# Cross-attention on one core: mask counts of blocks 4 to 7 in the values' bank, the projection directly behind the scores in odd steps

## The reference

```
q = heads(x @ W_Q.T); k = heads(ctx @ W_K.T); v = heads(ctx @ W_V.T)
scores = q @ k.T / 4;  scores = where(mask == 1, -1e9, scores)
p = softmax(scores);  out = concat_heads(p @ v) @ W_O.T + x
result = (out - mean(out)) * rsqrt(var(out) + 1e-5) * gamma + beta
```

## Time and profile before

| | us |
|---|---|
| three runs | 182.85, 186.15, 188.56 (median 186.15) |
| the profiled execution | 182.77 |
| its span, first to last instruction | 181.0 |
| PE busy | 159.6 (88%) |
| DVE busy | 136.9 (76%) |
| ACT busy | 103.2 (57%) |
| POOL busy | 102.5 (57%) |
| mean granted clock of PE | 0.976 |

### The profile page before, as it was taken

How to read it: one execution, slowest core, us unless ns; L and a number is a source line. 1 busy time by engine, 2 the same in 40 slices (tenths; PEclk the granted TensorE clock), 3 DMA queues, 4 the chain that set the end, 5 groups by cost and what they waited for, 6 DMA issues and landing times.

```text
span 181.0 us, 3572 instructions
## 1 busy us (share of the span) xinstructions
PE 159.6 (88%) x1224; PEld 87.9 (49%) x1224; DVE 136.9 (76%) x305; ACT 103.2 (57%) x188; POOL 102.5 (57%) x125
## 2 busy tenths in 40 slices
PE   7698877889579999999999999999999897999830
PEld 7455534444244565456545654565366462264520
DVE  0779755885958579788978897889989966748990
ACT  3224154673366565658765876587777659586400
POOL 7000761242835451448597959754954787865692
PEclk9999999999999999999999999999999999699995
DMA  4949947779867987973686665647551033020205
GB/s 158 384 120 184 257 86 224 182 167 230 188 170 217 281 237 216 253 201 85 196 274 181 193 198 145 187 164 205 141 182 53 4 121 116 0 116 4 116 0 232
DMA packets 21829, 30.17 MB, mean 167 GB/s; under 512 B 3436, under 2 KB 17356, under 8 KB 21812
## 3 DMA queue, kind: packets, MB, share of 16 engines
q1 hardware_dynamic: 20692, 28.19, 55.8%
q10 hardware_dynamic: 1120, 1.76, 2.9%
HBM read 11.28 MB, written 4.19 MB: 85 GB/s over the span
## 4 chain that ended last, share of the span: by engine, by line
PE 52%; DVE 12%; POOL 9%; issue 9%; DMA 8%; ACT 6%; ACTq 1%; POOLq 0%; SPq 0%; DVEq 0%
PE pv_ps L920 12%; PE work_ps L857 11%; PE work_ps L930 9%; PE scores_ps L912 9%; PE scores_ps L878 6%; DMA R<-neg_max_t 4%; DMA x_t<-in_x_cols 4%; POOL y L385 3%; DVE ctx_q L670 2%; PE scores_ps L857 2%; DVE neg_max L662 2%; DVE q L651 2%; POOL rstd L376 2%; POOL ctx_n L364 2%; DVE bn L690 1%
## 5 line engine op out<-in xcount | busy, mean ns | idle before, releaser
L547 ACT ACTIVATE probs<-scores_ps 77x512 f32<-77x512 f32 x108 | 57.7, 589 | 36.7 <-PE scores_ps L912 31.4
L662 DVE TENSOR_REDUCE neg_max<-scores_ps 128x6 f16<-128x462 f32 (+1 forms) x84 | 45.2, 565 | 11.0 <-PE scores_ps L878 11.0
L912 PE MATMUL scores_ps<-R,kb 126*77 126x512 f16 x128 | 39.5, 388 | 4.1 <-DMA R<-neg_max_t 3.0
L357 POOL TENSOR_TENSOR q<-q 128x512 f16<-128x512 f32 x14 | 16.2, 1161 | 43.4 <-ACT q L505 43.4
L878 PEld LDWEIGHTS scores_ps<-kb,R 125*128 125x128 f16 x512 | 26.7, 98 | 28.5 <-DVE neg_max L662 10.8
L920 PE MATMUL pv_ps<-probs,v_all 77*32 77x512 f32 x248 | 33.8, 618 | 2.2 <-ACT probs L551 1.0
L364 POOL TENSOR_TENSOR ctx_n<-ctx_q,rden 128x256 f32<-128x256 f32 x31 | 19.5, 628 | 23.6 <-DVE rden L672 23.5
L878 PE MATMUL scores_ps<-kb,R 125*128 125x77 f16 x512 | 31.2, 199 | 1.3 <-DVE neg_max L662 1.1
L670 DVE STREAM_TRANSPOSE ctx_q<-pv_ps 128x512 f32<-128x512 f32 x31 | 22.1, 712 | 9.3 <-PE pv_ps L920 8.9
L930 PE MATMUL work_ps<-wo_t,ctx_e 128*128 128x256 f32 x112 | 27.4, 388 | 0.0
L857 PE MATMUL work_ps<-x_t,wq_t 128*128 128x512 f32 x48 | 23.6, 614 | 0.4
(11 more groups left out here) (88 smaller groups left out, 158.7 us busy)
## 6 DMA issues: line engine op xcount, KB each, us to landing
R<-mask_t SPq DMA_DIRECT2D x12, 616.0 KB
R<-q SPq DMA_DIRECT2D x48, 128.0 KB
x_t<-in_x_cols SPq DMA_DIRECT2D x8, 512.0 KB, 6.2
y<-in_x SPq DMA_DIRECT2D x8, 512.0 KB, 4.6
out<-y SPq DMA_DIRECT2D x7, 512.0 KB, 2.6
mask_i<-in_mask_cols SPq DMA_DIRECT2D x8, 154.0 KB
out<-y ACTq DMA_DIRECT2D x2, 256.0 KB, 2.0
kb<-k SPq DMA_DIRECT2D x12, 38.5 KB, 2.9
```

The lines of the kernel that those rows point to most:

```text
L357: nc.gpsimd.tensor_tensor(q16[:, e, 1, :], q32[:, e, :], q16[:, e, 0, :], ALU.subtract).then_inc(q_low, 1)
L547: nc.scalar.activation(probs[:, s, head % 2, :], banks[0:KEYS, head % SCORES_RING, :], ACT.Exp).then_inc(exp_done, 1)
L662: nc.vector.tensor_reduce(to[:, t, lo:hi], max_ps[u % MAX_RING][:, 0:(hi - lo) * KEYS].rearrange("p (h k) -> p h k", k=KEYS), AX.X, ALU.ma ...
L912: nc.tensor.matmul(banks[0:KEYS, bank, :], kb[:, 2 * s + i, n // PER_BATCH, :], R[n % R_RING][:, 2 * s + i, :], start=True, stop=True).the ...
```

## The change

There are three edits. First, the counts of blocks 4 to 7 are written into pv_ps, the bank of the values, and not into work_ps; ACT's Sign reads them there. Second, such a count moves from step 0 of turns 1 to 4 to the very end of step 1, behind the projection and the units, with a wait for the transpose of the values before; the projection in step 1 takes over the wait for the residual and waits no longer for the Sign; instead values(n, 0) in step 2 wait for the Sign, since they overwrite the count. ACT's Sign moves from step 0 to step 1. Third, in odd steps of every turn from 1 on, no unit stands before: all stand behind, on PE and on DVE, in turns 5 and 6 as well.

```diff
+COUNTS_IN_WORK = 4
...
-    if s == nm_at(n) + 1:
+    if s == nm_at(n) + 1 or n > 0 and s % 2 == 1:
         before = 0
...
+        count_ps = [work_ps if m < COUNTS_IN_WORK else pv_ps for m in range(BLOCKS)]
...
-                nc.scalar.activation(not_full[m % 2][:, :], work_ps[:, :], ACT.Sign, bias=all_keys[:, :], scale=-1.0
+                nc.scalar.activation(not_full[m % 2][:, :], count_ps[m][:, :], ACT.Sign, bias=all_keys[:, :], scale=-1.0
...
                     elif n + 3 < N:
-                        if s == 0:
-                            if n == 1:
-                                q_hi(3, 1)
+                        if s == 0 and n == 1:
+                            q_hi(3, 1)
+                        if s == 1:
                             nf(n + 3)
...
-                nc.tensor.matmul(work_ps[:, :], ones16[:, :], eq16[m % 2][:, :], start=True, stop=True).then_inc(count_done, 1)
+                nc.tensor.matmul(count_ps[m][:, :], ones16[:, :], eq16[m % 2][:, :], start=True, stop=True).then_inc(count_done, 1)
...
                     if s == 0 and n >= 1:
                         values(n - 1, 3)
+                    if s == 2 and 1 <= n and n + 3 < N:
+                        pe.wait_ge(nf_ready, n + 4)
                     if s in (2, 4, 6):
                         values(n, s // 2 - 1)
...
                     if 1 <= n and n + 3 < N:
-                        if s == 0:
+                        if s == 1:
                             if n >= 2:
                                 pe.wait_ge(out_ready, 2 * (n - 1))
                             else:
                                 pe.wait_ge(q_scaled, 4 * HALVES)
-                            count(n + 3)
-                        if s == 1:
-                            pe.wait_ge(nf_ready, n + 4)
                             project_q(n + 3, 0, work_ps[:, :])
...
                     for m, u in behind:
                         max_unit(m, u)
+                    if s == 1 and 1 <= n and n + 3 < N:
+                        pe.wait_ge(pv_turned, QUADS * n)
+                        count(n + 3)
```

## The result

The changed kernel takes 186.01 us (median of 20 runs, 183.97 to 188.31), the kernel before 184.56 (20 runs, 182.85 to 188.56). Some executions of one and the same kernel are longer than others, so each ratio here compares only the runs within 1.5% of their kernel's fastest, while medians are of all runs. The ratio is 1.0073, 95% interval 1.0038 to 1.0109: slower by 0.7%, clear of the noise and within 2%. The profiled execution took 186.5 us with a span of 184.7.

What follows compares the result with a forecast made beforehand. PE's own work order was taken to set the pace in blocks 1 to 4, with DVE's queue order counting in 5 and 6. Terms 0.2 + 0 + 1.5 + 1.0 = +2.7 us on 184.5 gave 187.2 us, range 183.5 to 190.8.

Steps and rivals of the forecast that it cites:

- Count moved: Blocks 1 to 4: 0.27 taken out before the projection, 0.27 put in before the values; sum +0.2 us with block 1.
- Turn 1's new hole: Block 1 had no hole at the Sign and gets one before the values: +0.2 us.
- The low bound of this part, -0.7: Count move, blocks 1 to 4: lowest total, with -0.27 each if the Sign comes early enough to hide.
- DVE, turn 5: Block 5: DVE's new order delays u10 by 0.8 us and the transposes of the maxima by another 0.7; +1.5.
- The bound of 0.8: Block 5: low bound of its loss in us, if the statistics are covered after all.
- DVE, turn 6: Block 6: 1.67 us open before u10, the old 0.66 before u11 gone; net +1.0.
- Covers: Blocks 1 to 4: projection's wait for the residual, later mask product and SP's transfers stay hidden and cost nothing.
- The same matmuls in another order: Blocks 1 to 4, steps 1, 3 and 7: units run behind the projection instead of around it, 0 us.
- hidden Sign: Blocks 2 to 4: a period falling by 0.3 us would show the Sign hidden and the forecast wrong.
- (b): Not slower: Sign's hole closes, DVE's order harmless, u10 follows values in block 5 without a gap; 183.7 us, chance 0.17.
- (c): Holes only move on PE, and ACT's waits in blocks 5 and 6 absorb the stall; 184.7 us, chance 0.13.
- (d): Clock falls behind new holes in blocks 5 and 6, 1.7 us each; 188.9 us, or 190.6 with both; chance 0.20.

Runs made afterwards that it cites:

- e3: Changed kernel without its third edit, units in their old order and only the count moved; 184.96 us against 184.41 for the kernel before.
- e6: Changed kernel with step 1 of turns 5 and 6 back in its old order; 184.03 us in one run.
- e7: Kernel before with units behind in steps 3 and 7 of turns 1 to 4 only; 183.02 us against 184.47.
- e4: Changed kernel with the count directly behind the projection, ahead of the units, and units all behind only in turns 1 to 4; 183.93 us against 184.41.
- e2: Kernel before with the third edit alone, counts where they were; 188.75 us against 184.41 for the kernel before.
- e1: Changed kernel with the new unit order in turns 1 to 4 only, old order in turns 5 and 6; 183.56 us against 184.41 for the kernel before.
- e5: Kernel before with both units behind in step 1 of turns 5 and 6 only; 188.71 us against 184.47.
- e11: The kernel of e5 run once more; 186.54 us against 184.86 for the kernel before.
- e8: Kernel before, unchanged, run once more for its profile; 180.51 us in one run.
- e12: Changed kernel, unaltered, run once more; 187.59 us against 184.86 for the kernel before.
- e10: The kernel of e1 run once more; 184.19 us against 184.86 for the kernel before.

## Why the prediction was right, step by step

- **The whole:** +2.7 us forecast, on 184.5; measured +1.45 on 184.56. Direction, range and the "within 2%" were right, the size nearly double. That the base, half way through four executions, lies 0.06 from the median of twenty is luck, and the range of 7.3 us would have held every rival of the list, so it tested little; the turns did the testing.
- **Count moved:** 0 for turns 2 to 4 forecast, -0.04 each measured (e3). The hole of 0.27 went from the projection to the values, as worked out. Turn 1's new hole is there too (59.59 to 59.95 in the changed kernel at full clock, 0.26 beyond the usual 0.10). The low bound of this part, -0.7, does not come out of its terms: 0.2 - 3 x 0.27 is -0.6.
- **DVE, turn 5:** +1.5 forecast, +1.39 measured, in its two parts. u10 comes 0.79 later in its turn (0.8 forecast), and from u10 to the transposes it takes 0.60 longer (0.7 forecast). The profile's 0.41 there counts only from the modelled end of the values; from the start of the values to the transposes it is 1.47 (132.77 to 134.24) against 0.88 (129.24 to 130.12). The bound of 0.8, "if the statistics are covered", did not hold; e6 shows them uncovered.
- **DVE, turn 6:** +1.0 forecast, +0.92 measured; 1.66 open in front of u10 against 1.67, and the old wait given back.
- **Covers:** the SP queue, the mask product and the residual cost nothing, as said; e7 shows what the residual costs where its waiter is not moved.
- **The term it had wrong** is "The same matmuls in another order: two units in steps 1, 3 and 7 run behind the projection instead of around it, 0". It is worth -0.08 in each of three steps: e3 and the changed kernel differ by this edit alone, and turns 2 to 4 take 53.98 in the one and 53.31 in the other, -0.67 or -0.22 a turn. Over all four turns with projections the estimate is 12 x -0.08, so -0.9. With it the sum would have been +1.8; the ruler's +1.5 leaves turn 1 out, of which no profile of the changed kernel is at full clock throughout. The period of turns 2 to 4 fell by 0.26 a turn, close to the 0.3 that the prediction would have read as a hidden Sign; the Sign was not hidden.

Why a unit costs 0.08 more in front of a float32 product than behind it can be read from the weight loads. PEld and PE in step 3, in the kernel before (behind a unit) and in the changed one (behind the scores):

```profile
94.27 0.30 PEld L857 LDWEIGHTS work_ps<-x_t,wq_t 128*128 128x128 f32 x2
...
94.30 1.96 PE L857 MATMUL work_ps<-x_t,wq_t 128*128 128x512 f32 x4
96.10 0.60 PE L912 MATMUL scores_ps<-R,kb 126*77 126x512 f16 x2
```

```profile
97.02 0.41 PEld L860 LDWEIGHTS work_ps<-x_t,wq_t 128*128 128x128 f32 x2
...
97.23 1.88 PE L860 MATMUL work_ps<-x_t,wq_t 128*128 128x512 f32 x4
98.95 0.30 PE L881 MATMUL scores_ps<-kb,R 125*128 125x77 f16 x4
```

The first product starts at 94.30 in the one, 0.03 behind the start of its load, and at 97.23 in the other, 0.21 behind it: a load of 0.19 fits under a scores product of 0.21, not under a unit's of 0.035. This is a reading of the rows that fits; no run changed the load by itself. From there the projection takes 1.80 (94.30 to 96.10) against 1.72 (97.23 to 98.95). The rows of before held both figures; I had taken the sum of PE's work as independent of its order. The Trainium skill, TensorE: Matmul & The Clock Gate, Step-by-step: what each phase is for, says that the next tile's weights load while the current tile's matmul runs; the load behind the scores agrees, with its start 0.21 ahead of its product.

**Rivals:** (b) fell: u10 did not follow the values without a gap in turn 5. The gain of a hidden Sign exists (e4), but needs the count ahead of the units. (c) fell: ACT's waits absorbed nothing. (d) had the right price (1.7) and came true in one profile of e2's kernel; the two profiles of the changed kernel show no fall in turns 5 and 6, and how often one comes stays open.

## What to carry to other kernels

Two engines that follow one written order share its edits: check the order's effect on the second engine in the turns where the first has no long work to cover it. Here a limit on the turns (e1) keeps the gain and drops the loss, and moving the small producer ahead of the fillers (e4) makes them its cover. Try a float32 projection behind a long product and the short products behind it (here 0.08 us a projection). And cut profiles into turns before believing a median: 0.03 us is seen there, where medians of one kernel move by 0.6 to 2.2 us.

The best kernel of the study by its turns is e4's, 1.6 us under the kernel before in turns 2 to 4; by medians it is 0.5 and 1.1 under it, and e1's 0.85 and 0.67, so the times do not tell these two apart.

## What was not expected of the hardware

The spread of this kernel is falls of the clock at a few places: behind or within the wait for the maxima's transfer in turn 1 (2.9 us in e5 and e11), at 28 us in turn 0 (1.3 to 1.5), near the end (1.3) and, once, in turn 6 (1.7). The length of the transfer's wait itself varies, from 2.25 to 3.80 us. The same program has them in one execution and not in another. The length of the wait in front does not decide alone: in turn 1 the first profile of before kept 1.00 behind 3.0 us, e8 behind 2.2, while e6 fell to half behind 2.8 and e12 behind 2.7. The Trainium skill, TensorE: Matmul & The Clock Gate, What's actually happening, says that the point of the change varies from run to run since the monitor does not start with the kernel; e1 and e10, one program without and with a fall in turn 0, are in keeping with it, though they show whether a fall comes and not a shift of its time.
